# A fused transformer on one core: in the 32-wide causal attention the merges and statistics go to the end of VectorE's step, and in the ternary stage GpSimd's diagonals wait for the rounded codes

## The chip, the cores and the metric

One Trainium2 chip, one NeuronCore of it. The metric is the device time of one launch in microseconds. The kernel is one program that runs a whole chain of layers; all cross-engine order is written out by hand with semaphores.

## The reference

The input x is 16 x 256 x 128 (float32), with a context of 16 x 64 x 64. Eight layers are applied, each as `x = x + layer(layernorm(x), ...)`: four attentions and four feed-forward networks. Two of them matter here.

The third attention begins with a self-attention of 16 heads, 32 wide, on a normalised x. The mask comes after the softmax, so the sum of the softmax runs over all keys:

```python
xn = _ln(x, lnx_g, lnx_b); yn = _ln(y, lny_g, lny_b)
q, k, v = ...                        # 16 heads x 32
a = jax.nn.softmax(q @ k.T * 32 ** -0.5, axis=-1)
a = a * mask                         # keys up to the query's own
x_out = x + o @ li1_w + li1_b
```

The last layer is a feed-forward of two "bitlinear" products: weights rounded to -1, 0, 1, activations rounded to 8 bits per token by their largest absolute value:

```python
w_scale = clip(mean(abs(W)), EPS)
Wq = clip(round(W / w_scale), -1, 1) * w_scale
x_scale = clip(max(abs(x), axis=-1), EPS)
xq = clip(round(x * (127 / x_scale)), -128, 127) * (x_scale / 127)
h = gelu(xq @ Wq.T + b)              # and the same again with W2
```

## The kernel before

Thirteen stages follow each other, each with its own program for each engine: the start, then L0 attention `l0` and experts `l0f`, `l1s` and `l1c`, `l1f`, `a1` (the 32-wide causal attention), `a1_mlp`, `a2`, `a2_mlp`, `l2f`, `l3`, and the ternary network `l3f`. x stays in SBUF. All attentions but `a2` come from one function, `attention_rows`.

**The attention `a1`.** A batch of 256 tokens is worked on in U = 4 units of four heads; a step of every engine's loop serves one unit n, and 64 units run through it. `per_unit` is true where the heads are 32 wide, which is this stage alone. In a step, each engine does the following in this order (`at(k)` names the unit that is k steps ahead):

- TensorE: adds the negated maxima of unit n to its scores (`shift`, L528), computes the first half of the scores of n+1 (L490), its values (L468), multiplies the weights of n-1 with the values (`values`, L593 to L602), in one step out of four turns x (L444) and in another projects the output (L616), computes the second half of the scores (L490) and the transposed scores (L505) of n+1, and the queries and keys of n+2 (L454, L456). `psum_act` is shared by projections, values, turned x and output, so L454 also waits for the residual after an output projection.
- ScalarE: the exponentials (L673) and copies out of PSUM.
- GpSimd: four masks of the exponentials (`mask`, L1019), then what the plan has for it: `rstds` (L938, L940: variance plus epsilon, to the power -1/2) after the statistics, `gain` (L959, L962) after an apply, `gather` (an indirect DMA of expert rows, L950, with L946 before the first), and `preset` (L968).
- VectorE: `maxima` of the first half of n+1 (L815), the plan's work, the residual (L884) in one step out of four, `maxima` of the second half, and `normalise` of n-1 (L853 to L867).

The plan holds, for each batch, four gathers and four merges (`merge_choice`, L768: adds an expert's weighted row into x), and three layer norms, each with `ln_stats` (L783, L788) and `ln_apply` (L799). LEAD = 13 steps before the first unit of a batch the first gather is made, and each item has a fixed step. In the steady loop that gives four kinds of steps: one with apply 2, statistics 0, merge 0 and, beside them, the output projection and residual of an earlier batch; one with apply 0, statistics 1, merge 1 and the turn of x; one with apply 1 and merge 2; one with statistics 2 and merge 3. GpSimd's `rstds` stand in the step of the statistics, the apply one step later. All run in program order on their engines.

TensorE's `values` waits for the masks of its unit (`pm_ready`) and for the earlier `normalise`; its second half of scores waits for the first maxima; its `shift` waits for both maxima.

**The ternary network `l3f`.** 16 steps with two tiles of 128 tokens. On VectorE: statistics of a later pair of tiles (L2813, L2819), the largest absolute values of h and x (L2777, L2781), their clip, inverse and scaling (L2784, L2787, L2789, counted by `qstep`), the rounding of h (`hi`, L2794) and of x (`xi`, L2799), the factor `back` (L2805) and the scaled output (L2833). ScalarE takes the codes out of `hi` (L2956) and `xi`, does the GELU and the copies out of PSUM. GpSimd: rstd and shift of a later pair, a diagonal matrix of the inverses (`diag`, L2862) with which TensorE adds the bias two steps later, and the final addition to x (L2869).

Of the kernel before, what the change touches and what calls it, by code (L numbers as in the profile page):

```python
# [279 lines left out]
def attention_rows(nc, name, K, W, *, dh, units, x, out, after=None, norms=(), affine_q=None, affine_kv=None,  # L280
# [10 lines left out]
    U = units  # L291
    N = NB * U
    per_unit = C == 4
# [8 lines left out]
    plan, off = [], 0  # L302
# [8 lines left out]
    with ExitStack() as ctx:  # L311
# [104 lines left out]
        def inside(n, limit=N):  # L416
            return not isinstance(n, int) or 0 <= n < limit
# [322 lines left out]
        def _(dve):  # L740
# [20 lines left out]
            def merge_choice(b, par, i):  # L761
                k, t = i // TT, i % TT
                dve.wait_ge(gathered[par][i], 8 * (b - par) + 16)
                if k:
                    dve.wait_ge(merged, 2 * TT * b + TT)
                dve.sem_inc(K["passed"], 1)
                tile = x[:, bass.ds(b * TT + t, 1), :].rearrange("p a d -> p (a d)")
                dve.scalar_tensor_tensor(out=tile, in0=got[:, par, i, :],  # L768
                                         scalar=merge["p"][:, bass.ds(b * 2 * TT + 2 * t + k, 1)],
                                         in1=tile, op0=ALU.mult, op1=ALU.add).then_inc(merged, 1)  # L770
# [20 lines left out]
            def ln_apply(b, i):  # L791
                dve.wait_ge(rstd_ready[i], b + 1)
                src = (x if i == 0 else residual)[:, bass.ds(b * TT, TT), :]
                final = i == NLN - 1
                if final:
                    wait(dve, xn_turned, b)
                dst = xn if final else residual[:, bass.ds(b * TT, TT), :]
                for t in range(TT):
                    last = dve.tensor_scalar(dst[:, t, :], src[:, t, :], mv[:, i, t, 0:1], rstd[:, i, t:t + 1],  # L799
                                             ALU.subtract, ALU.mult)  # L800
                last.then_inc(xn_ready if final else scaled[i], 1)
# [49 lines left out]
            def normalise(idx, n, b, u):  # L851
# [16 lines left out]
                else:  # L868
# [2 lines left out]
                    dve.tensor_tensor(dst, rden[:, 1, :], add_t[:, bass.ds(b * T, T)], ALU.add)\  # L871
                       .then_inc(norm_done, 1)

            def residuals(b):
                dve.wait_ge(w_done, b + 1)
                view = psum_act[:, 0:T].rearrange("p (t d) -> p t d", t=TT)
                dst = out[:, bass.ds(b * TT, TT), :]
                base = dst
                if bob is not None:
                    dve.wait_ge(preset_done, b + 1)  # L880
                else:
                    base = (residual if residual is not None else x)[:, bass.ds(b * TT, TT), :]
                dve.sem_inc(K["passed"], 1)
                dve.tensor_tensor(dst, view, base, ALU.add).then_inc(res_done, 1)  # L884

            def emit(at):
                n, b, u, pos = at(0)
                n1, b1, u1, _ = at(-1)
                nw, bw, uw, _ = at(-2)
                nn, bn, un, posn = at(1)  # L890
                if inside(nn):
                    maxima(nn, posn, 0)
                for when, what, i in sorted(plan, key=lambda p: (-p[0], p[2])):
                    na, ba, ua, posa = at(LEAD - when)
                    if inside(na) and ua == 0:
                        if what == "merge":
                            merge_choice(ba, (posa // U) % 2, i)
                        elif what != "gather":
                            ln_stats(ba, i) if what == "stats" else ln_apply(ba, i)
                residual_now = inside(nw) and uw == U - 1 and store_t is None  # L900
                if residual_now and inside(nn):
                    residuals(bw)
                if inside(nn):
                    maxima(nn, posn, 1)
                    if before:
                        join_maxima(nn, posn)
                if paired and U == 1 and inside(n1):
                    turn_sums(n1, n1)
                    divide(n1)
                    turn_back(n1, b1)  # L910
                if paired and U == 4:
                    n3, b3, u3, _ = at(-3)
                    if inside(n1) and u1 == U - 1:
                        turn_sums(b1, n1)
                    if inside(nw) and uw == U - 1:
                        divide(bw)
                    if inside(n3) and u3 == U - 1:
                        turn_back(b3, b3)
                if not paired and inside(n1):
                    if per_unit or U == 1:  # L920
                        normalise(n1, n1, b1, u1)
                    elif u1 == U - 1:
                        normalise(b1, n1, b1, u1)
                if residual_now and not inside(nn):
                    residuals(bw)

# [1719 lines left out]
def ternary_mlp(nc, name, K, x, dst, W):  # L2646
# [13 lines left out]
    with ExitStack() as ctx:  # L2660
# [180 lines left out]
        @block.gpsimd  # L2841
        def _(pool):
            def emit(at):
                k, pk = at(4)
                if inside(k):
                    pool.wait_ge(stats, k + 1)
                    wait(pool, xn_ready, k - 1)
                    wait(pool, shift_ready, k)
                    pool.sem_inc(K["passed"], 1)
                    pool.tensor_scalar(veps[:], mv[:, pk % 2, :, 1], EPS, None, ALU.add).then_inc(pstep, 1)  # L2850
                    pool.tensor_scalar(nm[:], mv[:, pk % 2, :, 0], -1.0, None, ALU.mult).then_inc(pstep, 1)
                    pool.wait_ge(pstep, 2 * k + 2)
                    pool.tensor_tensor(rstd[:, pk % 2], veps[:], K["half"][:, 0:G], ALU.pow).then_inc(rstd_ready, 1)
                    pool.wait_ge(rstd_ready, k + 1)
                    pool.tensor_tensor(shift[:, pk % 2], nm[:], rstd[:, pk % 2], ALU.mult).then_inc(shift_ready, 1)
                q, pq = at(3)
                if inside(q):
                    pool.wait_ge(qstep, QS * q + 4)
                    wait(pool, h_done, G * (q - 3))
                    pool.sem_inc(K["passed"], 1)  # L2860
                    o = [P, G, P]
                    pool.tensor_tensor(diag[:, pq], K["ident"][:].unsqueeze(1).broadcast_to(o),  # L2862
                                       inverse[:, pq % 2, 1, :].unsqueeze(2).broadcast_to(o), ALU.mult).then_inc(diag_ready, 1)
                l, pl = at(-1)
                if inside(l):
                    pool.wait_ge(o1_ready, l + 1)
                    pool.sem_inc(K["passed"], 1)
                    dst = x[:, bass.ds(G * l, G), :]
                    pool.tensor_tensor(dst, o1[:, pl % 2], dst, ALU.add).then_inc(added, 1)  # L2869

            run(pool, emit)
# [256 lines left out]
```

## Time and profile before

| what | value |
|---|---|
| runs | 2459.04, 2466.41, 2468.11 us, median 2466.41 |
| profiled execution | 2461.6 us, span 2459.8 us |
| granted TensorE clock | 0.948 |
| busy, share of the span | TensorE 87%, VectorE 74%, ScalarE 54%, GpSimd 51% |
| `a1` | about 1,025 to 1,480 us of the span |
| `l3f` | about 2,355 to 2,460 us of the span |

Times in the rows are microseconds from the start of the span. A row of the timeline has start, duration, engine, line and operation, output and inputs, shape and count; instructions of one kind in a row are put together, and `[0.52 <-DVE x]` is idle time of that engine before them and what ended it. An instruction that waits for a port inside its execution shows it as a longer duration, not as idle time. PE is TensorE, DVE VectorE, ACT ScalarE, POOL GpSimd.

### The profile page before, as it was taken

What the parts mean: (1) busy time and instruction counts of PE and PEld (TensorE: products, weight loads), DVE (VectorE), ACT (ScalarE), POOL (GpSimd) and SP (SyncE); (2) the same over time, 40 slices, a digit from 0 to 9 for tenths busy, and PEclk for the clock granted to TensorE, in tenths of its full rate; (3) what the DMA queues carried; (4) which work ended last, traced back from release to release, by engine and by line L of the source; (5) the groups of instructions that cost most, each with busy time, mean ns of one, the idle gap of its engine ahead of it and who ended that gap; (6) DMA issues with size and microseconds to landing.
All of it is one profiled execution on the core that took longest, in us unless ns stands there. A gap on an engine that the chain in (4) does not pass through costs nothing. (4 is left out here: it accounts for less than half of the span.)

```text
span 2459.8 us, 67263 instructions
## 1 busy us (share of the span) xinstructions
PE 2128.7 (87%) x22352; PEld 1624.6 (66%) x22352; DVE 1813.6 (74%) x4599; ACT 1335.6 (54%) x2823; POOL 1248.3 (51%) x1940
## 2 busy tenths in 40 slices
PE   6869997999988779599999997899888999998866
PEld 4558995555656568566666666666667888886533
DVE  6975554666659766489999977688698866666987
ACT  3435552344335456355555556455476888884457
POOL 5547625555535367477777745333174334333433
PEclk9969998999999969899999999899999999999988
DMA  8032211000000223200000000000000311210000
GB/s 330 1 116 80 76 52 30 15 13 14 11 2 1 84 73 105 66 14 11 10 10 10 9 2 21 10 1 0 19 2 5 92 58 59 64 48 24 0 8 28
DMA packets 82432, 96.69 MB, mean 39 GB/s; under 512 B 16736, under 2 KB 61665, under 8 KB 80161
## 3 DMA queue, kind: packets, MB, share of 16 engines
q1 hardware_dynamic: 74016, 77.12, 9.8%
q0 software_dynamic: 8192, 16.79, 2.3%
q8 instruction: 115, 1.88, 0.3%
q14 instruction: 109, 0.89, 0.1%
HBM read 56.51 MB, written 37.36 MB: 38 GB/s over the span
## 5 line engine op out<-in xcount | busy, mean ns | idle before, releaser
L1729 DVE TENSOR_TENSOR l2f_h_lo<-l2f_h,l2f_h_hi 128x512 fp32r<-128x512 f32 x256 | 187.4, 764 | 100.9 <-ACT l2f_h_hi L1650 100.8
L1019 POOL TENSOR_TENSOR a_pm<-a_pt,tri_post 128x256 f32<-128x256 f32 x256 | 179.7, 732 | 73.1 <-ACT a_pt L673 72.7
L1657 ACT ACTIVATE l2f_h<-l2f_f,ahead 128x512 f32<-128x512 f32 x256 | 174.5, 689 | 49.5 <-DVE l2f_h_lo L1729 32.3
L815 DVE TENSOR_REDUCE l1s_negm<-l1s_s 128x6 bf16<-128x768 f32 x128 | 123.1, 962 | 95.3 <-PE l1s_s L490 95.2
L1824 POOL TENSOR_TENSOR l2f_acc<-l2f_tmp,l2f_acc 128x512 f32<-128x512 f32 x56 | 73.1, 1306 | 207.1 <-DVE l2f_tmp L1747 207.1
L673 ACT ACTIVATE l1s_pt<-l1s_st 128x768 f32<-128x768 f32 x128 | 96.9, 812 | 145.0 <-PE l1s_st L528 145.0
L815 DVE TENSOR_REDUCE a_negm<-a_s 128x4 bf16<-128x1024 f32 x128 | 156.2, 1220 | 24.6 <-PE a_s L490 24.5
L1650 ACT ACTIVATE l2f_h_hi<-l2f_h 128x512 fp32r<-128x512 f32 x256 | 154.5, 633 | 0.0
L673 ACT ACTIVATE a_pt<-a_st 128x1024 f32<-128x1024 f32 x128 | 126.3, 1062 | 2.6 <-PE a_st L528 2.6
L689 ACT ACTIVATE a_q_hi<-a_pa 128x256 bf16<-128x256 f32 x64 | 24.6, 384 | 185.7 <-PE a_pa L456 185.7
L1541 PE MATMUL l2f_f<-l2f_x_hi,l2f_w_hi 128*128 128x512 f32 x256 | 101.8, 398 | 1.2 <-POOL l2f_w_lo L1811 1.2
L1543 PE MATMUL l2f_f<-l2f_x_lo,l2f_w_hi 128*128 128x512 f32 x256 | 100.4, 392 | 0.0
L1541 PE MATMUL l2f_y<-l2f_h_hi,l2f_w_hi 128*128 128x512 f32 x256 | 100.4, 392 | 0.0
L1542 PE MATMUL l2f_f<-l2f_x_hi,l2f_w_lo 128*128 128x512 f32 x256 | 100.3, 392 | 0.0
L1543 PE MATMUL l2f_y<-l2f_h_lo,l2f_w_hi 128*128 128x512 f32 x256 | 99.7, 390 | 0.0
L1542 PE MATMUL l2f_y<-l2f_h_hi,l2f_w_lo 128*128 128x512 f32 x256 | 99.6, 389 | 0.0
L815 DVE TENSOR_REDUCE l_negm<-l_s 128x16 bf16<-128x1024 f32 x64 | 77.3, 1207 | 18.8 <-PE l_s L490 17.8
L2297 DVE SCALAR_TENSOR_TENSOR l0f_z<-l0f_bank_b,l0f_bt,l0f_a_s 128x128 f32<-128x128 f32 x144 | 43.9, 347 | 53.0 <-ACT l0f_a_s L2125 47.9
L505 PE MATMUL a_st<-a_q_f,a_k_f 32*128 32x256 f32 x1024 | 80.7, 392 | 0.3 <-ACT a_pt L673 0.3
L950 POOL DMA_INDIRECT a_got<-expert_rows,a_slot x64 | 68.3, 1067 | 22.8 <-POOL a_slot L946 13.0
L2367 POOL DMA_INDIRECT expert_rows<-l1f_xn,l1f_slots x64 | 63.7, 996 | 25.8 <-issue 11.8
L950 POOL DMA_INDIRECT l1s_got<-expert_rows,l1s_slot x64 | 65.1, 1018 | 22.0 <-POOL l1s_slot L946 12.2
(573 smaller groups left out, 6914.5 us busy)
## 6 DMA issues: line engine op xcount, KB each, us to landing
expert_rows<-zeros SPq DMA_DIRECT2D x16, 1056.0 KB, 17.4
l2f_wrow<-weights_by_expert SPq DMA_DIRECT2D x64, 256.0 KB, 3.2
l0f_w<-in_l0f_w SPq DMA_DIRECT2D x8, 640.0 KB, 9.7
l0f_x_in_sb<-expert_rows SPq DMA_DIRECT2D x72, 64.0 KB
expert_rows<-l0f_y SPq DMA_DIRECT2D x72, 64.0 KB, 1.6
l1f_x_in_sb<-expert_rows SPq DMA_DIRECT2D x72, 64.0 KB
expert_rows<-l1f_y SPq DMA_DIRECT2D x72, 64.0 KB, 1.9
ahead<-in_l2f_w SPq DMA_DIRECT2D x6, 512.0 KB, 4.6
```

What stands on the lines that cost most here:

```text
L505: pe.matmul(psum_st[:, i, kt * T:kt * T + T - q0], kb_f[rows(i), par_k, kt * P:(kt + 1) * P], q_f[rows(i), par_q, q0:T], start=kt == 0, st ...
L673: act.activation(pt[:, pos % 2, 2 * g:2 * g + 2, :], psum_st[:, 2 * g:2 * g + 2, 0:SC], ACT.Exp, scale=scale).then_inc(exp_done, 1)
L815: dve.tensor_reduce(dst, src, AX.X, ALU.max, negate=True).then_inc(max_done, 1)
L950: pool.indirect_dma_start(got[:, par, i, :], None, merge["rows"], bass.IndirectOffsetOnAxis(ap=slot[:, par, c:c + 1], axis=0))\
L1019: last = pool.tensor_tensor(pm[:, par, heads_, kt, :], pt[:, par, heads_, kt * (T + P):kt * (T + P) + P], K["tri_post"][:].unsqueeze(1).br ...
L1541: pe.matmul(dst, w_hi[:, wpar, cols], hi, start=start, stop=False)
L1542: pe.matmul(dst, w_lo[:, wpar, cols], hi, start=False, stop=False)
L1543: return pe.matmul(dst, w_hi[:, wpar, cols], lo, start=False, stop=stop)
L1650: act.activation(h_hi[:, pos % 2, j], h[:, j], ACT.Identity).then_inc(h_high, 1)
L1657: act.activation(h[:, j], psum_f[j][:], ACT.Gelu, bias=col(e, j)).then_inc(h_ready, 1)
L1729: dve.tensor_tensor(h_lo[:, pos % 2, j], h[:, j], h_hi[:, pos % 2, j].bitcast(F32), ALU.subtract)\
L1824: pool.tensor_tensor(acc[:, bass.ds(c * CH, CH)], tmp[:, pos % 2], acc[:, bass.ds(c * CH, CH)], ALU.add).then_inc(added, 1)
```

## The change

In `attention_rows`, the walk over the plan on VectorE becomes a function, `norms_of`, that is given the kinds of work to emit. For all attentions but `a1` it is called once with all kinds, in the old place. For `a1` the applies stay in the old place, between the first and the second maxima, and the merges and statistics are emitted at the end of the step, after the second maxima and `normalise` (in the step with a residual, after that too).

In `ternary_mlp`, GpSimd's diagonal of the pair q waits for `xi_ready` of q, the end of the rounding of x, where it waited for `qstep` at 4, the inverse.

```diff
+            def norms_of(at, kinds):
+                for when, what, i in sorted(plan, key=lambda p: (-p[0], p[2])):
+                    na, ba, ua, posa = at(LEAD - when)
+                    if inside(na) and ua == 0 and what in kinds:
+                        if what == "merge":
+                            merge_choice(ba, (posa // U) % 2, i)
+                        elif what == "stats":
+                            ln_stats(ba, i)
+                        else:
+                            ln_apply(ba, i)
+
...
                 if inside(nn):
                     maxima(nn, posn, 0)
-                for when, what, i in sorted(plan, key=lambda p: (-p[0], p[2])):
-                    na, ba, ua, posa = at(LEAD - when)
-                    if inside(na) and ua == 0:
-                        if what == "merge":
-                            merge_choice(ba, (posa // U) % 2, i)
-                        elif what != "gather":
-                            ln_stats(ba, i) if what == "stats" else ln_apply(ba, i)
+                norms_of(at, ("apply",) if per_unit else ("merge", "stats", "apply"))
...
                         normalise(b1, n1, b1, u1)
+                if per_unit:
+                    norms_of(at, ("merge", "stats"))
...
                 if inside(q):
-                    pool.wait_ge(qstep, QS * q + 4)
+                    pool.wait_ge(xi_ready, q + 1)
                     wait(pool, h_done, G * (q - 3))
```

## Rows read from the trace of the kernel before

**Rows 1.** Busy time, one period of a1: PE, PEld, DVE, ACT, POOL

```profile
1222.50:1249.40 26.90, 26.02 (x347) 18.45 (x343) 25.05 (x49) 14.33 (x31) 20.87 (x31) 1.00 0.04 10
```

**Rows 2.** Timeline of TensorE, one period of a1

```profile
1218.97 0.70 PE L454 MATMUL a_pa<-a_xq_t,ahead 128*128 128x256 f32 x2
...
1219.94 1.04 PE L528 MATMUL a_st<-ident_bf,a_negm 128*128 128x256 bf16 x8
...
1222.04 0.42 PE L593 MATMUL a_nd<-a_pm,a_v_f 128*32 128x128 f32 x8
...
1223.73 2.05 PE L616 MATMUL a_pa<-ahead,a_o_t 128*128 128x128 f32 x16
...
1227.50 0.67 PE L454 MATMUL a_pa<-a_xq_t,ahead 128*128 128x256 f32 x2 [0.52 <-DVE l_att L884]
...
1228.54 1.05 PE L528 MATMUL a_st<-ident_bf,a_negm 128*128 128x256 bf16 x8
...
1232.73 0.27 PE L490 MATMUL a_s<-a_kb_hi,a_q_hi 32*128 32x256 bf16 x2
...
1233.79 0.70 PE L454 MATMUL a_pa<-a_xq_t,ahead 128*128 128x256 f32 x2
...
1235.07 1.05 PE L528 MATMUL a_st<-ident_bf,a_negm 128*128 128x256 bf16 x8
...
1246.82 1.04 PE L528 MATMUL a_st<-ident_bf,a_negm 128*128 128x256 bf16 x8
```

**Rows 3.** Timeline of VectorE, the step with the output projection and after

```profile
1222.48 3.23 DVE L799 TENSOR_SCALAR a_xn<-l_base,a_mv,a_rstd 128x128 f32 x2
1225.63 0.47 DVE L783 BATCH_NORM_STATS2 a_st<-tokens_x 128x6 f32 x2
...
1226.92 0.42 DVE L884 TENSOR_TENSOR l_att<-a_pa,l_att 128x256 f32 x1
1227.27 1.22 DVE L815 TENSOR_REDUCE a_negm<-a_s 128x4 bf16<-128x1024 f32 x1
1228.40 0.44 DVE L853 STREAM_TRANSPOSE a_den_t<-a_nd 128x256 f32<-128x256 f32 x1
...
1229.95 1.23 DVE L815 TENSOR_REDUCE a_negm<-a_s 128x4 bf16<-128x1024 f32 x1
```

**Rows 4.** Timeline of GpSimd, two stretches of the same loop

```profile
1210.30 2.83 POOL L1019 TENSOR_TENSOR a_pm<-a_pt,tri_post 128x256 f32<-128x256 f32 x4 [1.12 <-ACT a_pt L673]
...
1217.41 2.84 POOL L1019 TENSOR_TENSOR a_pm<-a_pt,tri_post 128x256 f32<-128x256 f32 x4
...
1222.58 2.79 POOL L1019 TENSOR_TENSOR a_pm<-a_pt,tri_post 128x256 f32<-128x256 f32 x4
1226.69 0.36 POOL L938 TENSOR_SCALAR a_veps<-a_mv 128x2 f32<-128x2 f32 x1 [1.32 <-DVE a_mv L788]
...
1228.06 1.09 POOL L950 DMA_INDIRECT a_got<-expert_rows,a_slot  x1 [0.20 <-issue]
```

**Rows 5.** Timeline of a1's first batch, before its masks begin

```profile
1035.47 0.60 DVE L799 TENSOR_SCALAR l_base<-tokens_x,a_mv,a_rstd 128x128 f32<-128x128 f32 x2 [0.33 <-POOL a_rstd L940]
1035.63 1.12 POOL L950 DMA_INDIRECT a_got<-expert_rows,a_slot  x1 [0.20 <-issue]
```

**Rows 6.** Timeline of VectorE, a merge beside masks

```profile
1211.72 0.83 DVE L768 SCALAR_TENSOR_TENSOR tokens_x<-a_got,l1f_p,tokens_x 128x128 f32 x1
```

**Rows 7.** Ternary stage: timeline, then a line of VectorE's waits (us, times, longest)

```profile
2405.21 1.31 DVE L2794 TENSOR_SCALAR l3f_hi<-l3f_h,l3f_scaling 128x512 f32<-128x512 f32 x2
2405.23 0.61 POOL L2862 TENSOR_TENSOR l3f_diag<-ident,l3f_inverse 128x256 f32<-128x256 f32 x1 [0.29 <-DVE l3f_scaling L2789]
...
2412.12 1.15 ACT L2956 ACTIVATE l3f_hq<-l3f_hi,l3f_unround 128x1024 bf16<-128x1024 f32 x1 [0.83 <-DVE l3f_hi L2794]
...
2441.56 0.88 DVE L2794 TENSOR_SCALAR l3f_hi<-l3f_h,l3f_scaling 128x512 f32<-128x512 f32 x2
...
DVE l3f_mv L2819 <- DVE l3f_st L2813: 2.1, 11, 0.2
```

## The prediction

> **What bounds the kernel now.** I read the busy shares over stretches first, then the timeline of one period engine by engine, then the waits. The change touches two of thirteen stages. In the 32-wide causal attention (1,025 to 1,480 us) a batch of four steps takes 26.9 us, TensorE is busy for 26.0 of it and VectorE for 25.0 [rows 1]. Busy VectorE time holds waits inside instructions, so the timeline decides.
>
> I name the four steps of a period by what they hold beside the common work: D (apply 2, statistics 0, merge 0, output projection and residual), A (apply 0, statistics 1, merge 1, the turn of x), B (apply 1, merge 2), C (statistics 2, merge 3). A step runs from one start of the shift matmuls (L528) to the next: D 8.60, A 6.53, B and C 11.75 us together (5.79 and 5.96) [rows 2]; in all 26.88. What TensorE alone needs follows from the same rows. The Q/K projection (L454) comes 0.97 before a shift that nothing holds up. In A it starts 5.25 after the shift, so A could be 5.25 + 0.97 = 6.22. In D it waited 0.52 for the residual, and another 0.07 passed before the shift (1.04, not 0.97): 8.60 - 0.59 = 8.01. In B and C no matmul waits for VectorE, so they are at their own length. Own period: 8.01 + 6.22 + 11.75 = 25.98. At most 0.90 us a period can be won.
>
> The 0.90 has one cause: VectorE reaches the residual and the second maxima late. In D, the pair of L799 took 3.23 us [rows 3]; the same pair takes 0.60 where GpSimd gives way [rows 5]. The statistics and the merge behind it take 1.29 (L783 to L884), and only then come the residual and the maxima [rows 3]. The output projection had ended at 1223.73 + 2.05 = 1225.78 [rows 2], 1.14 before the residual began.
>
> **A rule beside that row.** L799 began at 1222.48, 0.10 before the first of four masks of GpSimd, and its pair ended 0.3 after the last of them [rows 3, 4]. The Trainium skill, page "SBUF — State Buffer", section "Who interferes with whom", says that the shared port pair is locked for one whole instruction, by whichever side starts first. The trace agrees that the engines exclude each other; it does not agree that the wait is one instruction long, or that 0.10 ahead wins. By the rule the wait would be at most one mask; the sum below doesn't use it.
>
> **Attention: what moves.** Nothing is added or removed. In each step the merge and the statistics go behind the second maxima and the normalisation; apply stays in front. No DMA is issued from VectorE; GpSimd's queue is not reordered, but it waits for the statistics (L938) with the gather and the next step's masks behind it, and TensorE's value matmuls wait for those masks. I walk one period, with A's shift at 0.
>
> - VectorE in D: second maxima start about 1.7 before A's shift (residual right after the projection), 1.13 later the normalisation, 1.55 later statistics 0 [rows 3]: 0.95. Its merge ends at 2.25, the first maxima take 1.13, apply 0 starts at 3.4.
> - GpSimd: the gather starts 2.43 after the statistics (1225.63 to 1228.06) [rows 3, 4]: 3.4, lasts 1.09. So apply starts at the start of the gather, not at its end. That is the place it has in the fill of the pipeline, where L799 started 0.16 before a gather and the pair ran in 0.60 [rows 5]. The long lock of 3.23 vanishes for all three applies. Masks A: 4.5 to 7.3.
> - VectorE in A: second maxima when the scores are there (1233.00 - 1228.54 [rows 2]), 4.5 (needed at about 5.7, so A gets its own 6.22); statistics 1 at 4.5 + 2.68 = 7.2. Gather at 9.6, masks B 10.75 to 13.55.
> - B: from the end of one set of masks to the start of the next, across gain, slot copy, gather and preset, 1217.41 - 1213.13 = 4.28 [rows 4]. Masks C start at 17.85 and end at 20.65.
> - TensorE needs masks C for the values of D, 2.10 after D's shift [rows 2]: 6.22 + 11.75 + 2.10 = 20.07. It waits 0.6. In the kernel before, those masks started at 1217.41 and were done 1.8 before the value matmuls of 1222.04 [rows 2, 4].
>
> So what is late next is GpSimd: it now waits for statistics at the end of two steps in a row and brings that lateness to D. Merge 2 and merge 3 also fall beside masks and take up to 0.83 each [rows 6], on a VectorE that then has room. Period: 25.98 + 0.6 = 26.58, 0.30 less than now. Twelve periods, from 1,088 to 1,384 us, have the gather and the long lock: 3.6 us. The ones at both ends, where GpSimd has fewer gathers, win 0.4 each from the shorter path, three of them: 1.2. Sum for this stage: **-4.8 us**. Bounds: the full 0.90 (12 x 0.90 + 1.2 = -12.0) if the masks arrive in time after all; a loss is bounded below, in the rivals.
>
> How gathers bear apply at their start: the row has 1.12 for the gather beside the pair, 1.09 without [rows 4, 5], and I take these 0.03 as nothing. The same page of the Trainium skill, under "A bandwidth-pool intuition that's wrong", warns that a GpSimd-issued DMA can't write its descriptors while VectorE runs a two-port instruction, and gives 3.1 us for one of 0.62. That speaks against the change; by it, gathers A and B would wait for the whole pair.
>
> **Ternary stage.** VectorE is the bound there. From 2,372 to 2,438 us the waits name nothing but its own earlier results in front of its instructions, 2.1 us in eleven waits for L2813 as the largest sum [rows 7]. The pair of L2794 takes 1.31 where GpSimd's diagonal (L2862, 0.61) starts 0.02 after it, and 0.88 at the end where there is no diagonal [rows 7]. Thirteen pairs are slowed, eight by 0.43 and five by 0.37: 5.3 us. With the wait on xi_ready the diagonal starts about 0.3 after the rounding of x, beside the two scaled adds that read PSUM (L2833); instructions of that kind are not slowed by GpSimd in the trace (L884 reads PSUM and ran in 0.42 beside L938) [rows 3, 4]. TensorE uses the diagonal two steps later, so nothing waits for it. Behind it in GpSimd's queue stand the final add and the next statistics' powers; they move by at most 0.1, and ScalarE's L2949 that needs them has slack. ScalarE waits 0.83 for L2794 in such a step [rows 7], so it can follow by 0.43; not every step leaves it so much, and I take 0.9 off the 5.3 for those that don't. Sum: **-4.4 us** (0, if the diagonal stalls the scaled adds by as much, to -5.3).
>
> **The sum.** -4.8 - 4.4 = -9.2 us. The profiled execution took 2461.6 (span 2459.8), so 2452.4 in its terms. The median of the three runs is 4.8 higher than it, and the forecast goes with the median: 2466.4 - 9.2 = **2457 us**, -0.37%. Within 0.5%, 12.3 us, this measurement can't tell a change from none.
>
> **Rivals.**
> 1. The masks are not late: a period takes 25.98. Time: 2466.4 - 12.0 - 4.4 = 2450. For it: GpSimd is busy for only 20.9 of 26.9 [rows 1] and my stall of 0.6 hangs on four small delays. Against: they add up in one queue in a fixed order.
> 2. An apply falls into the tail of a gather and is locked behind all four masks, as now, but in a worse place. It decides from about 0.6 us more delay in front of apply. If apply 2 alone: masks D end 7.8 after D's shift, the residual at 8.5, the maxima 9.9, the next shift 10.0 instead of 8.60; a period costs 10.0 + 6.22 + 11.75 = 27.97, +1.1, in all +13 - 4.4: 2475. If apply 0 or 1: their masks end 7.3 after the shift, the maxima about 8.9, the step takes 8.95 instead of 6.22: 12 x 2.4 = +29 - 4.4: 2491. For it: the margin is what now costs 2.6. Against: apply and gather hang on the same statistics, so their distance is fixed.
> 3. Gathers are held by apply for the length of the pair, 0.60, in A and in B: masks C come 1.2 later, D waits 1.8 instead of 0.6, a period is 27.8, +0.9: +11 - 4.4, 2473. Against: 1.12 beside the pair, 1.09 without [rows 4, 5]. The warning quoted above from the Trainium skill's page "SBUF — State Buffer" would do this.
> 4. The attention stage wins nothing, GpSimd's lateness eating 0.90, and only the ternary stage pays: 2462. Or the reverse, the ternary stage pays nothing, which gives the same number.
>
> **How the numbers follow.** Forecast 0.40; rival 1 0.25; rival 2 0.11 (half of it at 2475); rival 3 0.07; rival 4 0.17. Faster by over 0.5% (below 2454): rival 1 with a few forecast cases that run past the bound, 0.32. Slower by over 0.5% (above 2479): half of rival 2, and what noise of the three runs (9 us apart) and unlisted stalls add to the rest of rivals 2 and 3, 0.13. Within: 0.55. The range leaves out the far end of rival 2 and the noise below rival 1: 2445 to 2475.
>
> **What the profile after would show.** L799 of x_n: no duration near 2.97, all under 0.9. The projection's wait for the residual (0.52 now) gone. The values of D (L593) waiting for GpSimd's L1019 by about 0.6, and GpSimd waiting for L788 in A and D. Merges (L768) behind the normalisation, up to 0.83. L2794 pairs at 0.88, the ternary stage 4 us shorter. Wrong it would be if L799 still shows 2 to 3 us, if gathers grow beyond 1.2, or if the step A is above 6.5.

## The result, and the profile after

The changed kernel takes 2456.6 us (median of 20 runs, 2448.3 to 2464.3); the kernel before, run as often beside it, 2463.5. The ratio is 0.9971, 95% interval 0.9961 to 0.9981: 7 us, a real gain and smaller than the 0.5% bound. The profiled execution took 2457.0 us.

```profile
core 0: 2455.2 us, clock 0.947
```

Two stages had to be compared. Over the attention a1, from the first score matmul to the last mask, the trace has 428.6 us before and 426.3 after: -2.3. Over the ternary stage, from its first weight copy to its last scaled add, 101.6 before and 96.9 after: -4.7. Each of the two differences is part change and part this one execution.

In a1, 1.6 of the 2.3 us lie before the first shift matmul: 5.7 us before, 4.1 after. That stretch depends on when TensorE's granted clock rises. Kernels 5 and 11 below are the same program and have both lengths, here as busy time of PE, PEld, DVE, ACT, POOL and the granted clock (the 0.95 and 0.50) from the first score matmul to the first shift matmul, kernel 5 first:

```profile
1049.00:1053.10 4.10, 3.43 (x34) 2.32 (x34) 3.47 (x5) 0.86 (x3) 2.72 (x5) 0.95 0.06 16
```

```profile
1076.00:1082.10 6.10, 5.92 (x35) 3.98 (x34) 3.58 (x5) 0.89 (x3) 3.81 (x6) 0.50 0.03 11
```

At 0.50, the lower of the clock's two levels, the stretch is 2 us longer with the same work; the kernel before has 0.54 there and the changed one 0.91. Why it rises earlier in one execution is not shown. So the attention's own gain is read in the loop, from the first shift to the last: 418.3 us before, 417.6 after, **-0.7**.

In the ternary stage the first thirteen steps, those with a slowed pair, take 68.8 us before and 63.7 after: **-5.1**. The traces without the ternary change (before, kernels 1 and 6) agree in these steps to 0.1 us, though their whole stage takes 101.6, 103.3 and 102.8: in the step behind them VectorE waits 0.78 us in the first and 2.46 in the other two for a product of TensorE. The two parts are thus 5.8 of the measured 7 us. The rest is no larger than what the stages in between vary by, which the change does not touch: 873.8 to 880.9 us in the fourteen traces.

**One period of a1** (busy time of PE, PEld, DVE, ACT, POOL from shift to shift; answers to [rows 1]):

```profile
1217.03:1243.83 26.80, 25.80 (x339) 18.66 (x338) 20.57 (x48) 14.31 (x30) 20.81 (x31) 1.00 0.04 10
```

VectorE's busy time fell from 25.05 to 20.57 us though none of its work was removed: the difference is waiting inside instructions, 2.6 of it in the one pair of L799 below. The period fell only from 26.91 to 26.80 (mean of five). That is the first lesson of this profile: busy time that holds waits for a port does not tell the bound, and relieving VectorE of 4.5 us bought 0.1.

**TensorE, a step D of the period** (timeline; answers to [rows 2]; in the changed kernel the residual is L895, and GpSimd's lines and those of the ternary stage stand 7 further down):

```profile
1216.06 0.70 PE L454 MATMUL a_pa<-a_xq_t,ahead 128*128 128x256 f32 x2
...
1217.03 1.04 PE L528 MATMUL a_st<-ident_bf,a_negm 128*128 128x256 bf16 x8
...
1218.49 0.71 PE L468 MATMUL a_pa<-ahead,a_xkv_t 128*128 128x128 f32 x4
1219.79 0.42 PE L593 MATMUL a_nd<-a_pm,a_v_f 128*32 128x128 f32 x8 [0.58 <-POOL a_pm L1026]
...
1221.47 2.05 PE L616 MATMUL a_pa<-ahead,a_o_t 128*128 128x128 f32 x16
...
1224.64 0.70 PE L454 MATMUL a_pa<-a_xq_t,ahead 128*128 128x256 f32 x2
...
1225.61 1.04 PE L528 MATMUL a_st<-ident_bf,a_negm 128*128 128x256 bf16 x8
```

The wait of L454 for the residual (0.52 before) is gone. In its place the value matmuls L593 wait 0.58 for GpSimd's masks. From shift to shift the steps are now D 8.54 to 8.58, A 6.32, B 5.96, C 5.95; before they were 8.59 to 8.71, 6.53, 5.79, 5.96.

**VectorE and GpSimd, the same stretch** (timelines; answer to [rows 3] and [rows 4]):

```profile
1220.74 0.59 DVE L799 TENSOR_SCALAR a_xn<-l_base,a_mv,a_rstd 128x128 f32 x2
1223.84 0.42 DVE L895 TENSOR_TENSOR l_att<-a_pa,l_att 128x256 f32 x1 [2.51 <-PE a_pa L616]
...
1229.26 0.60 DVE L799 TENSOR_SCALAR l_base<-tokens_x,a_mv,a_rstd  x2
```

```profile
1217.45 2.09 POOL L1026 TENSOR_TENSOR a_pm<-a_pt,tri_post 128x256 f32<-128x256 f32 x3
...
1220.77 1.08 POOL L957 DMA_INDIRECT a_got<-expert_rows,a_slot  x1 [0.20 <-issue]
1221.89 2.77 POOL L1026 TENSOR_TENSOR a_pm<-a_pt,tri_post 128x256 f32<-128x256 f32 x4
1227.92 0.37 POOL L945 TENSOR_SCALAR a_veps<-a_mv 128x2 f32<-128x2 f32 x1 [3.26 <-DVE a_mv L788]
...
1229.30 1.09 POOL L957 DMA_INDIRECT a_got<-expert_rows,a_slot  x1 [0.20 <-issue]
...
1233.96 0.37 POOL L945 TENSOR_SCALAR a_veps<-a_mv 128x2 f32<-128x2 f32 x1 [0.78 <-DVE a_mv L788]
```

The pair of L799 takes 0.59, not 3.23, and begins with the gather. VectorE now waits 2.51 for the projection. GpSimd waits 3.26 and 0.78 for statistics in D and A, with gather and masks queued behind: that lateness arrives at L593.

One long lock is left, in the first batch, where a set of masks begins 0.03 ahead of the apply (GpSimd, then VectorE):

```profile
1060.69 2.78 POOL L1026 TENSOR_TENSOR a_pm<-a_pt,tri_post 128x256 f32<-128x256 f32 x4
1060.72 3.10 DVE L799 TENSOR_SCALAR a_xn<-l_base,a_mv,a_rstd 128x128 f32<-128x128 f32 x2
```

**The ternary stage, one step** (timelines of VectorE, ScalarE and GpSimd; answers to [rows 7]):

```profile
2403.21 0.88 DVE L2801 TENSOR_SCALAR l3f_hi<-l3f_h,l3f_scaling 128x512 f32<-128x512 f32 x2
2404.01 0.48 DVE L2806 TENSOR_SCALAR l3f_xi<-l3f_xn,l3f_scaling 128x128 f32<-128x128 f32 x2
...
2404.48 0.61 DVE L2840 SCALAR_TENSOR_TENSOR l3f_o<-l3f_po,l3f_back,ahead 128x128 f32<-128x128 f32 x2
...
2408.35 0.88 DVE L2801 TENSOR_SCALAR l3f_hi<-l3f_h,l3f_scaling 128x512 f32<-128x512 f32 x2
```

```profile
2404.53 1.15 ACT L2963 ACTIVATE l3f_hq<-l3f_hi,l3f_unround 128x1024 bf16<-128x1024 f32 x1
```

```profile
2404.74 0.61 POOL L2869 TENSOR_TENSOR l3f_diag<-ident,l3f_inverse 128x256 f32<-128x256 f32 x1 [2.12 <-DVE l3f_xi L2806]
```

Every rounding pair (L2801, L2794 before) takes 0.88. The diagonal (0.61) lies beside the scaled adds and the statistics; the adds keep their 0.61. A step takes 5.13 (2408.35 - 2403.21), where a step with a slowed pair took 5.57.

### The profile page after: what moved, and what is told of

Read it like the earlier page. It is cut to its first block and busy times, and to the rows that moved or that the text cites. A ratio compares the mean times of both kernels' runs of the same rounds, so it can differ in the third digit from the quotient of the medians.

```text
span 2455.2 us, 67255 instructions
## 1 busy us (share of the span) xinstructions
PE 2129.7 (87%) x22352; PEld 1629.9 (66%) x22352; DVE 1762.3 (72%) x4599; ACT 1336.1 (54%) x2823; POOL 1245.0 (51%) x1940
## 5 line engine op out<-in xcount | busy, mean ns | idle before, releaser
L673 ACT ACTIVATE l1s_pt<-l1s_st 128x768 f32<-128x768 f32 x128 | 96.9, 812 | 144.8 <-PE l1s_st L528 144.8
L505 PE MATMUL a_st<-a_q_f,a_k_f 32*128 32x256 f32 x1024 | 79.6, 388 | 0.3 <-ACT a_pt L673 0.3
L2057 PE MATMUL l0f_bank_g<-l0f_z,l0f_w 128*128 128x128 f32 x576 | 76.9, 277 | 0.0
```

The source lines that it names most:

```text
L505: pe.matmul(psum_st[:, i, kt * T:kt * T + T - q0], kb_f[rows(i), par_k, kt * P:(kt + 1) * P], q_f[rows(i), par_q, q0:T], start=kt == 0, st ...
L673: act.activation(pt[:, pos % 2, 2 * g:2 * g + 2, :], psum_st[:, 2 * g:2 * g + 2, 0:SC], ACT.Exp, scale=scale).then_inc(exp_done, 1)
L2057: last = pe.matmul(bank_g[j % 2][:, g * P:(g + 1) * P], w2[:, j % 2, blk * P:(blk + 1) * P], z[:, j % 2, i, :], start=i == 0, stop=i == 1)
```

## The experiments

Steps are given as D/A/B/C, from one start of L528's first matmul to the next; a period is the mean of five of them. The loop of a1 is the time from its first shift to its last, which leaves the clock at the stage's start out. Times of 5 to 8 are single executions, so there the steps decide. Diffs stand against the changed kernel unless said otherwise. Kernels 9 to 12 ran on a chip on which the kernel before takes 2487.4 us, so their ratios count; the changed kernel itself was not timed there. The one program traced on two chips (5 and 11) has a period of 26.18 on both.

**1 and 2. Each half alone.** Attention part only:

```diff
-                    pool.wait_ge(xi_ready, q + 1)
+                    pool.wait_ge(qstep, QS * q + 4)
```

> Only the attention's part of the change (GpSimd's diagonal waits for the inverse as before). Theory: the traces of before and after differ by 2.3 to 3.0 us in this stage and by 4.7 us in the ternary stage, so this kernel gives -2.5 us, ratio 0.999. Rival, the forecast's sum: -4.8 us, ratio 0.998. Rival, the stage's start and end moved by run-to-run noise and the order is worth nothing: 1.000. Period of the attention 26.79 us, as after.

Measured: 2464.0 us against 2464.0, ratio 0.9993 [0.9979, 1.0007]. Period 26.79, steps 8.55/6.32/5.95/5.96; loop 417.6 us, ternary stage 103.3.

Ternary part only (against the kernel before):

```diff
-                    pool.wait_ge(qstep, QS * q + 4)
+                    pool.wait_ge(xi_ready, q + 1)
```

> Only the ternary stage's part. Theory: the pair of roundings of h takes 0.88 instead of 1.31 us in thirteen steps, the stage is 4.7 us shorter, ratio 0.998. Rival: part of the 4.7 us came from the earlier stages (another clock state of TensorE at the start of the stage), then less than 3 us. Attention period 26.88, as before.

Measured: 2458.8, ratio 0.9978 [0.9967, 0.9990]. Period 26.91, loop 418.4, ternary stage 96.6 and 63.5 in its thirteen steps. The two ratios multiply to the whole one, 0.9971. The ternary part is most of the gain. The attention part alone can't be told from none by time; in the trace its loop is 0.7 to 0.8 us shorter. The expectation for the attention (-2.5) took the stage's whole difference for the change's; most of it was the clock at the stage's start.

**3 and 4. Statistics or merges last, not both.** The kinds ahead of the second maxima and behind the normalisation, first for kernel 3, then for kernel 4:

```diff
-                norms_of(at, ("apply",) if per_unit else ("merge", "stats", "apply"))
+                norms_of(at, ("merge", "apply") if per_unit else ("merge", "stats", "apply"))
...
-                    norms_of(at, ("merge", "stats"))
+                    norms_of(at, ("stats",))
```

```diff
-                norms_of(at, ("apply",) if per_unit else ("merge", "stats", "apply"))
+                norms_of(at, ("stats", "apply") if per_unit else ("merge", "stats", "apply"))
...
-                    norms_of(at, ("merge", "stats"))
+                    norms_of(at, ("merge",))
```

> The whole change, but in the attention only the statistics go last; merges stay between the maxima. Theory: what breaks the long lock of the apply of x_n is that the reciprocal roots, and with them the gather, now come late, so that the apply falls at the gather's start. Then no apply is near 2.95 us, the value matmuls of step D wait for the masks, and the period is 26.7 to 26.9 us as after. Rival: it is the sum of work between the maxima that counts, merges as well; then the period lies between 26.88 and 26.79 in proportion and some apply stays long.

Measured: 2459.7, ratio 0.9975 [0.9962, 0.9988], period 26.78, steps as in the changed kernel, mask wait 0.54. No apply takes 2.95, one takes 2.20. The loop is 419.9 us, 1.6 longer than before: at its start the shift waits 1.27 and 1.43 us for the second maxima. With statistics last alone the attention wins nothing.

> The whole change, but in the attention only the merges go last; statistics stay between the maxima. Theory: the order of gather, apply and masks stays as in the kernel before, so the apply of x_n keeps its 2.95 us in twelve periods; the residual comes only a merge (0.3 us) sooner and the value matmuls don't wait for masks: period 26.5 to 26.7. Rival: the lock goes as well because the first maxima start a merge later, behind the first mask: apply 1.4 us, period near 26.2.

Measured: 2451.4, ratio 0.9948 [0.9929, 0.9966]; period 26.40, steps 8.26/6.22/5.95/5.95; loop 411.8 us. The long lock stayed, as expected; the period is a little below the 26.5 of the theory. VectorE and TensorE, one step D:

```profile
1219.27 3.20 DVE L799 TENSOR_SCALAR a_xn<-l_base,a_mv,a_rstd 128x128 f32 x2
...
1223.35 0.42 DVE L895 TENSOR_TENSOR l_att<-a_pa,l_att 128x256 f32 x1
```

```profile
1218.79 0.42 PE L593 MATMUL a_nd<-a_pm,a_v_f 128*32 128x128 f32 x8
1223.92 0.67 PE L454 MATMUL a_pa<-a_xq_t,ahead 128*128 128x256 f32 x2 [0.20 <-DVE l_att L895]
```

What follows: with the merge out of the way of the maxima, the long lock (3.20) can stay and costs only what remains of the residual's lateness: L454 waits 0.20, D is 8.26 instead of 7.94, and A gets 0.10 of that back (6.22 instead of 6.32). The masks are in time. The statistics' move is what takes the lock away, and it brings the mask wait, which is dearer. Merges last alone shorten the loop by 6.5 us; with the statistics moved as well 0.7 are left. By time the intervals of this kernel (four runs) and of the changed one still touch.

**5 and 11. GpSimd's gather ahead of the reciprocal roots.** If GpSimd's wait for statistics is what delays the masks, work that doesn't need them should go first:

```diff
-                for when, what, i in sorted(plan, key=lambda p: (-p[0], p[2])):
+                first = (lambda p: p[1] != "gather") if per_unit else (lambda p: False)
+                for when, what, i in sorted(plan, key=lambda p: (first(p), -p[0], p[2])):
```

> The changed kernel, with GpSimd's gather emitted before the reciprocal roots of the same step (attention only). It takes the gather out of the path from the statistics to the masks: masks C come some 1.9 us earlier, and the wait of the value matmuls in step D (0.58 us in after) is gone. But now masks follow the roots directly, so the applies start beside masks. Theory, gathers shield the applies: they show 0.7 us or more each instead of 0.34, and where one starts ahead of the first mask it is locked for the burst (2.9 us). Short waits: period 26.2 to 26.5 us. Long ones in A or B: period 28 or more. Rival, an apply waits for one mask at most wherever it falls: never over 0.8 us.

Measured, one execution of each: 2444.6 beside 2464.6; period 26.18, steps 7.94/6.33/5.97/5.94. GpSimd's timeline from the end of one set of masks to the next, twice, and the value matmuls:

```profile
1217.10 2.77 POOL L1026 TENSOR_TENSOR a_pm<-a_pt,tri_post 128x256 f32<-128x256 f32 x4
1220.05 1.08 POOL L957 DMA_INDIRECT a_got<-expert_rows,a_slot  x1 [0.17 <-issue]
1223.84 0.36 POOL L945 TENSOR_SCALAR a_veps<-a_mv 128x2 f32<-128x2 f32 x1 [2.70 <-DVE a_mv L788]
1224.29 0.72 POOL L947 TENSOR_TENSOR a_rstd<-a_veps,half 128x2 f32<-128x2 f32 x1
1225.00 2.77 POOL L1026 TENSOR_TENSOR a_pm<-a_pt,tri_post 128x256 f32<-128x256 f32 x4
```

```profile
1225.17 1.32 DVE L799 TENSOR_SCALAR l_base<-tokens_x,a_mv,a_rstd  x2
```

```profile
1215.69 0.43 PE L593 MATMUL a_nd<-a_pm,a_v_f 128*32 128x128 f32 x8
```

The gather fits into GpSimd's wait, the masks follow the roots at once, and L593 waits for nothing. Applies fall inside masks and take 1.3 a pair, not 3.2; no single one takes over 0.77, as the rival had it.

> The same kernel as e5_gather_first, timed in five rounds: in the attention's steps GpSimd issues its gather ahead of the reciprocal roots. Theory (GpSimd's wait for the statistics delays the gather and with it the masks; the delay is what the change pays for the long lock that it takes away): about 2445 us, ratio to the kernel before 0.992 to 0.994, period 26.21, causal masks of step D no longer waited for. Rival (the one look was a lucky execution and the order of gather and roots does nothing): 2456, ratio 0.997.

Measured: ratio 0.9942 [0.9926, 0.9958], period 26.18. That is below the changed kernel's interval (0.9961 to 0.9981, from another chip) too, and the loop is 409.6 and 409.7 us in the two traces against 417.6: the order of GpSimd's queue was worth as much as the whole change. On the first chip it would be about 2449, an estimate from the ratio. The expected 0.992 to 0.994 was just missed.

**6 and 7. GpSimd made short, in both kernels.** The causal mask is left out of the values; GpSimd's four masks multiply 4 of 128 columns. So VectorE's order is seen without contention and without late masks.

```diff
-                                    last = pe.matmul(dst[:, 0:P], lhs, pm[:, par, i, 0, :], start=True, stop=False,
+                                    last = pe.matmul(dst[:, 0:P], lhs, p[:, 0:P], start=True, stop=False,
...
-                    last = pool.tensor_tensor(pm[:, par, heads_, kt, :], pt[:, par, heads_, kt * (T + P):kt * (T + P) + P],
-                                              K["tri_post"][:].unsqueeze(1).broadcast_to([P, 2, P]), ALU.mult)
+                    last = pool.tensor_tensor(pm[:, par, heads_, kt, 0:4], pt[:, par, heads_, kt * (T + P):kt * (T + P) + 4],
+                                              K["tri_post"][:, 0:4].unsqueeze(1).broadcast_to([P, 2, 4]), ALU.mult)
```

> The kernel before, with the causal mask of the attention left out of the result: GpSimd's mask instructions work on 4 of 128 columns into a tile nobody reads, and the value matmuls read the unmasked exponentials. Everything else runs. It shows the stage's period with no long GpSimd instruction in VectorE's way. Theory: the order on VectorE is worth nothing of itself, and the period is TensorE's with ScalarE's copies, 26.17 us (D 7.94, A 6.32, B and C 5.95), as the last three periods of after have it. Forecast's reading: 25.98 us. Rival, the order itself matters: over 26.4.

Measured: 2449.6, period 26.17, steps 7.94/6.33/5.95/5.96.

> The same edit in the changed kernel (causal mask left out of the result). Theory: GpSimd is no longer late with masks, the wait of 0.58 us in step D is gone and the period is 26.17 us, the same as with this edit in the kernel before. Rival: D stays at 8.55 because something other than the masks holds it.

Measured: 2449.9, period 26.17, steps 7.94/6.32/5.96/5.95. Both orders give the same steps: in these kernels VectorE's order of instructions matters only through GpSimd, and the loop is 409.5 us in both. And TensorE's own period is 26.17, not 25.98.

The trace of the kernel before had this number: its last batches have no lock and no late residual. TensorE there, from step B of the last disturbed batch on:

```profile
1396.26 1.05 PE L528 MATMUL a_st<-ident_bf,a_negm 128*128 128x256 bf16 x8
1397.56 0.71 PE L468 MATMUL a_pa<-ahead,a_xkv_t 128*128 128x128 f32 x4
...
1402.05 1.04 PE L528 MATMUL a_st<-ident_bf,a_negm 128*128 128x256 bf16 x8
1403.52 0.71 PE L468 MATMUL a_pa<-ahead,a_xkv_t 128*128 128x128 f32 x4
...
1408.01 1.04 PE L528 MATMUL a_st<-ident_bf,a_negm 128*128 128x256 bf16 x8
...
1415.94 1.04 PE L528 MATMUL a_st<-ident_bf,a_negm 128*128 128x256 bf16 x8
...
1422.27 1.04 PE L528 MATMUL a_st<-ident_bf,a_negm 128*128 128x256 bf16 x8
...
1434.18 1.04 PE L528 MATMUL a_st<-ident_bf,a_negm 128*128 128x256 bf16 x8
```

From 1408.01 to 1434.18 a period takes 26.17. In step B behind the late shift (1396.26, a step of 5.79) L468 starts 1.30 after the shift, in C (1402.05, 5.96) 1.47.

**8. Where the 0.19 comes from.** On top of kernel 7, ScalarE's copy of k (L692) takes 4 of 256 columns, so most of k is left out of the transposed scores (L505):

```diff
-                    act.activation(k_f[:, par, :], psum_act[:, T:2 * T], ACT.Identity).then_inc(proj_out, 1)
+                    act.activation(k_f[:, par, 0:4], psum_act[:, T:T + 4], ACT.Identity).then_inc(proj_out, 1)
```

> As e7, and ScalarE's last copy of the projected keys takes 4 of 256 columns, the rest of the tile being zero from the start (the transposed scores are wrong, the work of all other instructions the same). Theory: what I took for TensorE's own length of a step is held by ScalarE's four copies out of the shared PSUM bank, which the next values' projection (L468) waits for; then it starts 0.1 us or more earlier in every step and the period falls from 26.17 to between 25.5 and 25.9 us. Rival, TensorE alone sets it: 26.17 stays.

Measured: 2441.7, period 25.49, steps 7.76/6.15/5.78/5.8. In the changed kernel ScalarE copies q and k out of the tile a_pa in a row. L468 writes the same tile and waits for the semaphore that the last copy counts (`proj_out`); it begins 0.05 after that copy:

```profile
1217.23 0.38 ACT L689 ACTIVATE a_q_hi<-a_pa 128x256 bf16<-128x256 f32 x1 [2.63 <-PE a_pa L456]
...
1218.04 0.40 ACT L692 ACTIVATE a_k_f<-a_pa 128x256 f32<-128x256 f32 x1
```

L468 then starts 1.46 after the shift (1218.49 - 1217.03). With the short copy:

```profile
1214.19 1.04 PE L528 MATMUL a_st<-ident_bf,a_negm 128*128 128x256 bf16 x8
1215.48 0.71 PE L468 MATMUL a_pa<-ahead,a_xkv_t 128*128 128x128 f32 x4
```

1.29, and each of the four steps is 0.15 to 0.18 shorter. So ScalarE's copies stand in TensorE's own step. The 0.17 by which L468 starts earlier here is also what it has in the short step B of the kernel before (1.30 instead of 1.47): there the late shift had given the copies time. To let L468 wait for q's copies alone was not tried: the copy of k would read the bank that L468 writes.

**9. Slot copy a gather earlier**, so that its wait leaves step B:

```diff
+                def copy_slots(b, par):
...
+                if i == 0 and (not per_unit or (isinstance(b, int) and b == 0)):
+                    copy_slots(b, par)
...
+                if per_unit and i == 2 * TT - 1 and not (isinstance(b, int) and b + 1 >= NB):
+                    copy_slots(b + 1, 1 - par)
```

> The changed kernel with GpSimd's copy of the next batch's eight slot numbers put behind the fourth gather of the batch before, so that the wait and copy of about 1 us no longer stand between two mask bursts in step B. Theory (GpSimd as a whole is late after the waits for statistics in D and A and the 1 us in B is lateness that it could give back): the 0.58 us wait for masks in step D goes, period 26.2, a1 about 7 us shorter than the changed kernel, about 2450 us, ratio 0.9945. Rival (the lateness is made anew in C by the wait for statistics 2, whatever happened in B): nothing changes, 2456, ratio 0.997.

Measured: ratio 0.9954 [0.9937, 0.9971], period 26.58; loop 414.5. The mask wait did go, and in every second batch a lock took its place: D is 7.94 and A 6.82 in one, D 8.33 and A 6.22 in the other. VectorE and GpSimd in the first:

```profile
1243.66 2.21 DVE L799 TENSOR_SCALAR a_xn<-l_base,a_mv,a_rstd 128x128 f32 x1
```

```profile
1243.69 2.77 POOL L1032 TENSOR_TENSOR a_pm<-a_pt,tri_post 128x256 f32<-128x256 f32 x4
```

0.03 ahead of the masks, apply was held for three of them. Both expectations had missed this.

**10. Only statistics 0 last.**

```diff
-                    if inside(na) and ua == 0 and what in kinds:
+                    if inside(na) and ua == 0 and (what in kinds or (what, i) in kinds):
...
-                norms_of(at, ("apply",) if per_unit else ("merge", "stats", "apply"))
+                norms_of(at, ("apply", ("stats", 1), ("stats", 2)) if per_unit else ("merge", "stats", "apply"))
...
-                    norms_of(at, ("merge", "stats"))
+                    norms_of(at, ("merge", ("stats", 0)))
```

> The changed kernel with the merges last and, of the statistics, only those of normalisation 0 last (step D); statistics 1 and 2 stand between the maxima as before, so that GpSimd's roots in A and C find them ready. Theory (the late statistics of A and C make the masks late, and the statistics of D, moved last, take the lock away): period 26.1 to 26.3, no wait for masks in D, 2447 to 2451 us, ratio 0.994. Rival (the apply of normalisation 1 in B, now 0.3 to 0.5 us earlier or later against GpSimd, falls into a gather's tail and takes the lock of 3 us there): period 26.7 or more, 2456 or more.

Measured: ratio 1.0004 [0.9991, 1.0016], period 27.24, loop 425.7. The rival came; of the theory only the end of the mask wait. D has its own 7.94, A takes 6.43 to 6.93, B 6.82 to 7.12. Step B:

```profile
1267.08 1.09 POOL L957 DMA_INDIRECT a_got<-expert_rows,a_slot  x1 [0.20 <-issue]
1268.20 2.76 POOL L1026 TENSOR_TENSOR a_pm<-a_pt,tri_post 128x256 f32<-128x256 f32 x4
```

```profile
1267.55 2.83 DVE L799 TENSOR_SCALAR l_base<-l_base,a_mv,a_rstd  x2
```

```profile
1271.57 1.05 PE L528 MATMUL a_st<-ident_bf,a_negm 128*128 128x256 bf16 x8 [0.81 <-DVE a_negm L815]
```

Apply 1 begins 0.47 into the gather, its second half runs into the masks, the second maxima are late and the shift waits 0.81. In D the pair of x_n still took 3.24 there, so moving statistics 0 alone doesn't take that lock away, which I had expected it to; kernel 3 moves all three and does. Statistics 2, on which apply 2 waits, is the likely one, but it was not moved alone.

**12. Kernels 5 and 9 together** (both diffs).

> Both: gather ahead of the reciprocal roots in a step, and the slot copy a gather earlier. If GpSimd's lateness is already gone with the gather first, the second edit adds nothing: period 26.2, 2444 to 2446 us, ratio 0.9925, the same as e11. If GpSimd still holds the own period through the slot copy in B, the period falls further, below 26.0, and the time to 2441 or less. If the gathers, issued still earlier, meet an apply at their tail, a lock of 3 us comes back and the time is 2455 or more.

Measured: ratio 0.9951 [0.9935, 0.9967], five runs, period 26.18, steps 7.94/6.32/5.98/5.94. The same as kernel 5, though not the 0.9925 expected for both: with the gather first, GpSimd no longer sets the period, which is TensorE's own 26.17 but for 0.01.

## Why the prediction was right, step by step

The time came out at 2456.6 against 2457. That it came so close is in part luck: the gain was 6.8 us where 9.2 were forecast, and the starting point, the median of three runs, was 2.9 above the median of twenty. The signs were right in both stages; the attention won 0.7 instead of 4.8, the ternary stage 5.1 instead of 4.4.

- **The long lock vanishes.** Right. All pairs of L799 in the steady part take 0.59 to 1.01 (31 pairs from 1,100 to 1,380 us), and gather and apply begin together. One of the kind that the prediction called a sign of being wrong (2 to 3 us) is there all the same, 2.84 in the first batch.
- **The projection's wait for the residual goes.** Right: 0.52 to none, and A fell to 6.32.
- **GpSimd's lateness makes a new stall of 0.6 at L593.** Right in place and size: 0.58. Kernels 5 and 9, which take it away in two ways, and 4, where the statistics stay early, show that the late statistics are its cause.
- **Gathers bear apply at their start.** Right: the 42 gathers beside which an apply runs take 1.08 to 1.14, and their data land a median of 2.67 us after the start; in the kernel before it is 2.65 for the gathers without an apply beside them. The warning of the Trainium skill's page "SBUF — State Buffer", section "A bandwidth-pool intuition that's wrong", does not show in these rows.
- **The rule set beside [rows 3, 4].** The prediction counts the apply's 0.10 ahead of the first mask as a start ahead of GpSimd. But GpSimd was not idle then; its gather ran until 1222.55:

```profile
1221.46 1.09 POOL L950 DMA_INDIRECT a_got<-expert_rows,a_slot  x1 [0.20 <-issue]
```

So that row speaks against the rule only by the length of the wait, four masks and not one instruction.

- **Attention -4.8.** Mis-sized: -0.7 in the loop (kernel 1, with this part alone: 0.7 to 0.8). The term that failed is the own period, "8.01 + 6.22 + 11.75 = 25.98". Kernels 6 and 7 measure 26.17. I took the 5.79 of step B as B's own length. It was the length of a step after a late shift: A's 6.53 and B's 5.79 make 12.32, and after 6.32 and 5.96 make 12.28. ScalarE's copies let no undisturbed step follow faster, so most of A's gain is B's loss. So the room was 26.91 - 26.17 = 0.74 a period and the stall took back 0.6. Ten full periods win 0.16 each, 1.6 in all. The second term that failed is the 1.2 us to be won at both ends: there the loop loses 0.9, in the steps before the first period (0.1), in the first one (27.02 instead of 26.49, with a mask wait of 0.78) and in the last (26.81 instead of 26.54).
- **Ternary -4.4.** Measured -5.1 in the thirteen steps. The mechanism was right. The 0.9 set aside for steps in which ScalarE can't follow was hardly needed; the bound of 5.3 was nearer.
- **Rival 1** (masks in time) was a real possibility, only by an edit elsewhere: with it, kernel 5 has 26.18. **Rival 2** (an apply locked in a gather's tail) came in this kernel only once, in the first batch; it came in every second batch of kernel 9 and in every batch of kernel 10, with B longer by 0.9 to 1.2 in the latter (2.7 had been reckoned for a step). The row for it was sound, the price too high. **Rival 3** is refuted by the gathers' 1.08 to 1.14. **Rival 4** (GpSimd's lateness eats the attention's gain and only the ternary stage pays) is closest to what the attention did: -0.7 us in the loop, ratio 0.9993, not told from none. Its time, 2462, was 5 us off, 2.9 of it by the starting point.

## What to carry to other kernels

Before pricing a reordering, measure the length that a step would have without the disturbance, by shrinking the other engine's work or in batches of the same trace that are not disturbed (here the last ones); a short step behind a late one is a debt paid back and not its own length. Compare stages from a point at which the clock is the same in both traces, and look at traces of unchanged code for how far a stage moves by itself. When work is moved later on one engine, look at which engine waits in order for its result and what is queued behind that wait: here to move independent work (the gather) ahead of it was worth as much as the change itself. An instruction's place against another engine's bursts is a matter of tenths of a microsecond or less, so a small edit elsewhere can bring a lock back, and only the timeline shows it.

## What the hardware showed that I had not expected

**Where a tensor_scalar of VectorE starts beside GpSimd decides what it costs.** Taken over the eleven traces with whole masks, each instruction of L799 in a1 that starts during a gather which masks follow at once (none starts between 0.47 and 0.71):

```
start after the gather's    instructions    duration, us
0.10 to 0.23 us             148             0.33 to 0.35
0.27 to 0.47 us              41             0.69 to 0.91
0.71 to 1.09 us              52             2.22 to 3.29
```

The last row reaches to the third or fourth of the masks. Where no masks follow, the four that start later than 0.25 take 0.34 to 0.43. Of the 494 that start within the masks 490 take 0.34 to 0.82. The other four start within 0.03 us of the first mask's start and take 2.19 to 2.85 (two more that start as early take 0.78), and fourteen that start in the 0.03 us between gather and masks take 2.19 to 2.88. So the second of a pair that begins well into a gather is in danger, and the margin is a few tenths of a microsecond.

The Trainium skill, page "SBUF — State Buffer", section "Who interferes with whom", has the port pair locked for one whole instruction by whoever starts first. The 2.21 us of an apply that began 0.03 ahead of the masks (kernel 9) do not agree with it: by that rule it should have run first, in 0.34. A lead of 0.03 is small for such rows, so this alone is weak. The firmer disagreement is the length: a wait of three or four masks is not one instruction. Why a burst is let through whole in the one case and cut in the other, these traces do not show.
